# Six-stage transformer kernel: layer norms row tile by row tile, with their deviations made by GpSimd

## The reference

```
ln(x)  = (x - mean(x)) / sqrt(var(x) + 1e-5)        # over the last axis
x = x + L0_xattn(ctx, ctx, ln(x), mask, ...)        # 16 heads of 32, masked cross attention
x = x + L0_attn(ln(x), ...)                         # ln again with gain g and bias b, selective scan
x = x + L0_ffn(ln(x), ...)                          # shared expert and 2 of 8 experts
x = x + L1_xattn(ln(x), ctx, ctx, ...)              # 16 heads of 32, cross attention
x = x + L1_attn(ln(x), ...)                         # linear attention with cos and sin positions
x = x + L1_ffn(ln(x), ...)                          # see below
# L1_ffn(x): qkv = x @ w_qkv; causal attention o; h = ln(x + o) * g1 + b1
#            2 of 8 experts give moe; return ln(h + moe) * g2 + b2
```

## Time and profile before

| | |
|---|---|
| median of 3 runs | 4477.82 us (4474.61 to 4483.54) |
| the profiled execution's own time | 4484.0 us |
| its span | 4481.9 us |
| mean granted TensorE clock | 0.93 of full |
| busy: TensorE, VectorE, ScalarE, GpSimd | 3975.0, 2993.9, 2351.9, 1667.8 us |

### The profile page before, as it was taken

The page is one execution under the profiler, slowest core; times in us unless marked ns, Lnnn a source line. Parts: engine busy times, 40 slices in busy tenths (PEclk is TensorE's granted clock), DMA queues, the critical chain, the costliest instruction groups (busy, mean ns, idle before and its releaser), DMA issues. The chain is left out here.

```text
span 4481.9 us, 50984 instructions
## 1 busy us (share of the span) xinstructions
PE 3975.0 (89%) x17680; PEld 2213.4 (49%) x17680; DVE 2993.9 (67%) x3608; ACT 2351.9 (52%) x3611; POOL 1667.8 (37%) x984
## 2 busy tenths in 40 slices
PE   7995899999999686678999779999999988769997
PEld 6883344444443341147777434444444335447775
DVE  4333878777785359936777567777778644467776
ACT  2221577777777333313676426666666631337674
POOL 0001487778878425400000036666566630000000
PEclk9997899999999779889999869999999988789998
DMA  8998566666666200022888546666666540318886
GB/s 310 328 336 273 150 153 152 155 154 148 156 149 144 80 14 0 0 85 113 302 301 302 203 132 154 152 154 152 140 151 144 120 99 26 79 59 305 304 300 227
DMA packets 301550, 751.69 MB, mean 168 GB/s; under 512 B 55793, under 2 KB 89329, under 8 KB 268016
## 3 DMA queue, kind: packets, MB, share of 16 engines
q1 hardware_dynamic: 245136, 560.20, 37.1%
q0 software_dynamic: 47456, 171.46, 19.0%
q10 hardware_dynamic: 8704, 16.78, 1.1%
HBM read 484.23 MB, written 98.37 MB: 130 GB/s over the span
## 5 line engine op out<-in xcount | busy, mean ns | idle before, releaser
L749 ACT ACTIVATE prob<-psum 128x512 f32<-128x512 f32 x1552 | 891.7, 595 | 430.7 <-PE psum L647 393.7
L647 PE MATMUL psum<-q_stack,k_ring 98*128 98x512 f32 x2048 | 1006.1, 510 | 19.8 <-ACT prob L749 14.4
L924 POOL TENSOR_TENSOR den_pool<-den_pool,prob 128x1024 f32<-128x1024 f32 x372 | 937.2, 2519 | 220.2 <-DVE den_pool L836 184.7
L622 PE MATMUL psum<-k_ring,q_stack 96*128 96x512 f32 x2048 | 691.7, 422 | 106.3 <-DVE row_max L807 36.1
L803 DVE TENSOR_REDUCE row_max<-psum 128x1 f32<-128x1024 f32 x512 | 615.3, 1220 | 238.0 <-PE psum L622 235.0
L807 DVE CUSTOM_DVE_ANT_0 psum<-psum,mask_q 128x1024 f32<-128x1024 f32 x512 | 627.3, 1233 | 206.5 <-PE psum L622 191.2
L647 PEld LDWEIGHTS psum<-q_stack,k_ring 98*128 98x128 f32 x2048 | 395.2, 194 | 620.7 <-ACT prob L749 274.7
L1891 DVE TENSOR_TENSOR weight_lo<-weight_raw,weight_hi 128x2048 fp32r<-128x2048 f32 x240 | 546.9, 2289 | 163.2 <-ACT weight_hi L1834 162.9
L665 PE MATMUL psum<-prob,x 128*32 128x512 f32 x3104 | 515.7, 610 | 0.9 <-ACT prob L749 0.9
L622 PEld LDWEIGHTS psum<-k_ring,q_stack 96*128 96x128 f32 x2048 | 394.1, 200 | 213.7 <-issue 84.2
L1834 ACT ACTIVATE weight_hi<-weight_raw 128x2048 fp32r<-128x2048 f32 x240 | 454.4, 1916 | 43.2 <-DMA weight_raw<-in_L_ffn_w 25.3
(11 more groups left out here) (422 smaller groups left out, 6385.6 us busy)
## 6 DMA issues: line engine op xcount, KB each, us to landing
weight_raw<-in_L_ffn_w SPq DMA_DIRECT2D x120, 1024.0 KB, 6.7
den_dma<-prob POOLq DMA_DIRECT2D x204, 512.0 KB, 4.9
k_ring<-k_hi SPq DMA_DIRECT2D x1024, 64.0 KB, 2.2
weight_raw<-in_L_ffn_Wu SPq DMA_DIRECT2D x60, 1024.0 KB, 7.2
weight_raw<-in_L_ffn_Wd SPq DMA_DIRECT2D x60, 1024.0 KB, 4.9
den_dma<-xnT POOLq DMA_DIRECT2D x68, 512.0 KB, 4.9
k_ring<-k_lo SPq DMA_DIRECT2D x512, 64.0 KB, 2.4
ctxT<-in_ctxT SPq DMA_DIRECT2D x16, 1024.0 KB, 9.5
```

The source lines that it names most:

```text
L622: ins = e.matmul(max_banks(q)[:, a * KC:(a + 1) * KC], q_stack[h % n_q][0:QROWS, i * P:(i + 1) * P], k_ring[0:QROWS, (n + a) % kring, :], ...
L647: e.matmul(k.bank(b % 2), k_ring[:, n % kring, kt * P:(kt + 1) * P], q_stack[h % n_q][:], start=not masked, stop=True, skip_group_check=ma ...
L749: e.activation(prob[b // 2 % n_p][:, b % 2, :], k.bank(b % 2), ACT.Exp, scale=scale).then_inc(s_exp, 1)
L924: e.tensor_tensor(den[:], den[:], tile, ALU.add).then_inc(s_dpool, 1)
```

## The change

Each norm works row tile by row tile. GpSimd makes the deviation of a tile, as (var + eps) to the power -0.5, so that ScalarE's Sqrt and VectorE's reciprocal go. VectorE's list interleaves statistics, aggregates and rows of neighbouring tiles. TensorE transposes a row tile (its four squares into one bank) as soon as that tile is there; ScalarE, and in the context preparation and the scan input VectorE as before, copies the bank into xnT with columns strided by chunk. Where gain and bias are applied on the way (scan input), VectorE's 4 copies of 128x512 become 16 of 128x128. The diff, cut:

```
-        v.tensor_scalar(self.rstd[:], self.mv[:, :, 1], 1e-5, None, ALU.add).then_inc(self.s_var, 1)
-    def act_root(self, a):
-        a.wait_ge(self.s_var, 1)
-        a.activation(self.rstd[:], self.rstd[:], ACT.Sqrt).then_inc(self.s_root, 1)
+    def pool_rstd(self, g):
         for i in range(TT):
+            g.wait_ge(self.s_mean, i + 1)
+            g.tensor_scalar(self.rstd[:, i:i + 1], self.mv[:, i, 1:2], 1e-5, None, ALU.add).then_inc(self.s_eps, 1)
+            g.wait_ge(self.s_eps, i + 1)
+            g.tensor_tensor(self.rstd[:, i:i + 1], self.rstd[:, i:i + 1], self.k.minus_half[:], ALU.pow
+                            ).then_inc(self.s_rstd, 1)
...
+    def dve_rows(self, v, dst, src, done=None):
+
+        def row(i):
+            v.wait_ge(self.s_rstd, i + 1)
             v.tensor_scalar(dst[:, i, :], src[:, i, :], self.mv[:, i, 0:1], self.rstd[:, i:i + 1], ALU.subtract,
                             ALU.mult).then_inc(self.s_rows, 1)
+        for i in range(2):
+            self.dve_stats(v, src, i, done)
+        for i in range(TT):
+            self.dve_mean(v, i)
+            if i + 2 < TT:
+                self.dve_stats(v, src, i + 2, done)
+            if i > 0:
+                row(i - 1)
+        row(TT - 1)
...
     def pe_turn(self, p, src):
 
-        p.wait_ge(self.s_rows, TT)
-        for c in range(DT):
-            if c >= 2:
-                p.wait_ge(self.s_xT, c - 1)
-            for i in range(TT):
-                ins = p.transpose(self.k.bank(c % 2)[:, i * P:(i + 1) * P], src[:, i, c * P:(c + 1) * P],
+        for i in range(TT):
+            p.wait_ge(self.s_rows, i + 1)
+            if i >= 2:
+                p.wait_ge(self.s_xT, i - 1)
+            for c in range(DT):
+                ins = p.transpose(self.k.bank(i % 2)[:, c * P:(c + 1) * P], src[:, i, c * P:(c + 1) * P],
                                   self.k.ident[:])
             ins.then_inc(self.s_turned, 1)
...
+    def act_turned(self, a, dst):
+
+        for i in range(TT):
+            a.wait_ge(self.s_turned, i + 1)
+            a.activation(dst[:, :, i * P:(i + 1) * P], self.turned(i), ACT.Copy).then_inc(self.s_xT, 1)
...
+    def dve_turned_gained(self, v, dst, gain):
+        for i in range(TT):
+            v.wait_ge(self.s_turned, i + 1)
+            for c in range(DT):
+                ins = v.tensor_scalar(dst[:, c, i * P:(i + 1) * P], self.turned(i)[:, c, :], gain[:, 0, c:c + 1],
+                                      gain[:, 1, c:c + 1], ALU.mult, ALU.add)
+            ins.then_inc(self.s_xT, 1)
```

`dve_rows_gained` is interleaved in the same way, with its first pass (`scaled`) right behind each tile's aggregate. The edits in the lists:

```
     # scan_inputs, GpSimd
+                first.pool_rstd(e)
+                second.pool_rstd(e)
                 for c in range(DT - 1):
                     e.wait_ge(s_whi, c + 1)
                     e.tensor_tensor(w_part[1][:, c, :], w[:, c, :], w_part[0][:, c, :].bitcast(F32), ALU.subtract
...
     # scan_inputs, VectorE
-                e.wait_ge(first.s_rows, TT)
-                second.dve_variance(e, xn)
-                second.dve_rows(e, xm, xn)
+                second.dve_rows(e, xm, xn, done=lambda i: e.wait_ge(first.s_rows, i + 1))
                 e.wait_ge(s_c, 64)
-                second.dve_turned(e, k.xnT, gain=col)
+                second.dve_turned_gained(e, k.xnT, col)
...
     # l1_cross, ScalarE
-                        norm.act_root(e)
                         e.wait_ge(s_wq3, 16)
                         for c in range(DT):
                             e.activation(wq[:, c, :].rearrange("p (h n) -> p h n", n=DH), wq3[:, c, :, 0:DH], ACT.Copy
                                          ).then_inc(s_wq, 1)
+                        norm.act_turned(e, k.xnT)
                         q.act(e)
...
     # l0_experts, ScalarE
-                    norm.act_root(e)
                     ex.act_first_split(e)
+                    norm.act_turned(e, k.xnT)
                     ex.act_x(e, norm.s_xT)
...
     # l1_linear, ScalarE: after the exponentials, ahead of the silu copies
+                norm.act_turned(e, k.xnT)
                 e.wait_ge(s_pairs, 2)
...
     # causal_projections, ScalarE
-                norm.act_root(e)
+                norm.act_turned(e, k.xnT)
...
     # causal_to_routes, ScalarE
                     bias.act(e)
-                    norm.act_root(e)
-                    e.wait_ge(norm.s_rows, TT)
+                    norm.act_turned(e, k.xnT)
                     rows.act(e)
```

More of the change, by code:

```diff
@@ L128, in _ @@
             e.memset(k.ones[:], 1.0)
+            e.memset(k.minus_half[:], -0.5)
             e.wait_ge(s_zero, 2)
@@ L170, in dve_rows, with dve_stats, dve_mean @@
-    def dve_rows(self, v, dst, src):
-        v.wait_ge(self.s_root, 1)
-        v.reciprocal(self.rstd[:], self.rstd[:]).then_inc(self.s_rec, 1)
-        v.wait_ge(self.s_rec, 1)
-        for i in range(TT):
+    def dve_stats(self, v, src, i, done):
+        if done is not None:
+            done(i)
+        v.bn_stats(self.stats[:, i, :], src[:, i, :]).then_inc(self.s_stats, 1)
+    def dve_mean(self, v, i):
+        v.wait_ge(self.s_stats, i + 1)
+        v.bn_aggr(self.mv[:, i, :], self.stats[:, i, :]).then_inc(self.s_mean, 1)
@@ L182, in dve_rows_gained, with scaled, row @@
+        row(TT - 1)
+    def dve_rows_gained(self, v, dst, src, gain, plus, done=None):
+        def scaled(i):
             v.scalar_tensor_tensor(out=src[:, i, :], in0=src[:, i, :], scalar=self.mv[:, i, 0:1], in1=gain,
                                    op0=ALU.subtract, op1=ALU.mult).then_inc(self.s_scaled, 1)
-        v.wait_ge(self.s_root, 1)
-        v.reciprocal(self.rstd[:], self.rstd[:]).then_inc(self.s_rec, 1)
-        v.wait_ge(self.s_rec, 1)
-        for i in range(TT):
+        def row(i):
+            v.wait_ge(self.s_rstd, i + 1)
@@ L190, in dve_rows_gained @@
                                    op0=ALU.mult, op1=ALU.add).then_inc(self.s_rows, 1)
-    def pe_turn(self, p, src):
-        p.wait_ge(self.s_rows, TT)
-        for c in range(DT):
-            if c >= 2:
-                p.wait_ge(self.s_xT, c - 1)
-            for i in range(TT):
-                ins = p.transpose(self.k.bank(c % 2)[:, i * P:(i + 1) * P], src[:, i, c * P:(c + 1) * P],
+        for i in range(2):
+            self.dve_stats(v, src, i, done)
+        for i in range(TT):
+            self.dve_mean(v, i)
+            if i + 2 < TT:
+                self.dve_stats(v, src, i + 2, done)
+            v.wait_ge(self.s_mean, i + 1)
+            scaled(i)
+            if i > 0:
+                row(i - 1)
@@ L341, in _ @@
                 e.memset(m4[:], 0.0).then_inc(s_clear, 1)
+                norm.pool_rstd(e)
             @block.scalar
@@ L1005, in _ @@
                         k.clear_old(e)
+                    @block.gpsimd
+                    def _(e):
+                        norm.pool_rstd(e)
                     @block.vector
@@ L1086, in _ @@
             def _(e):
-                first.dve_variance(e, k.x)
                 first.dve_rows(e, xn, k.x)
-                e.wait_ge(first.s_rows, TT)
-                second.dve_variance(e, xn)
-                second.dve_rows(e, xm, xn)
+                second.dve_rows(e, xm, xn, done=lambda i: e.wait_ge(first.s_rows, i + 1))
                 e.wait_ge(s_c, 64)
-                second.dve_turned(e, k.xnT, gain=col)
+                second.dve_turned_gained(e, k.xnT, col)
                 for c in range(DT):
@@ L1137, in _ @@
             def _(e):
-                first.act_root(e)
                 for c in range(DT):
```

54 lines of the change are left out of this document (16 added, 38 removed).

## The result

The change is slower. Over nine runs each the changed kernel has a median of 4496.59 us (4488.13 to 4505.9), the kernel before 4478.0 us (4472.78 to 4485.88); the ratio is 1.0036, interval 1.0024 to 1.0049, so +16 us (18.6 between the medians). I had forecast 4477 us and a range up to 4488; 0.12 was my chance for slower. The profiled execution took 4496.59 us, its span is 4494.9, its mean granted clock 0.928. The page of after answers to the earlier trace rows: TensorE is busy 13.6 us longer although it does the same matmuls, VectorE 11.6 us less, GpSimd 34.8 us more.

A forecast was written before the change was run, and what follows sets the result against it. TensorE, busy 89% of the span, was taken as the bound, so only its waits for norms counted. Gains in scan input and before the router, mostly given back elsewhere, summed to -0.9 us: 4477 us forecast, range 4469 to 4488.

The forecast's parts named there:

- if the two cross attentions [...] change their length: Sign of being wrong: the cross attentions, some 2,200 us together and untouched by the diff, change length.
- P: Context preparation: VectorE's wait for the root goes, but nothing ahead of TensorE waited for it; 0 us.
- S: Scan input, two norms: in_proj_lo subtractions start later, yet TensorE's fourth group starts sooner; -4.4 us.
- L: In each norm, time from a bn_aggr's end until VectorE may use the tile's deviation; taken as 0.6 us.
- X: Shared expert: ScalarE's copies of the transposes stand behind its weight casts, so TensorE starts later; +1.4 us.
- C: Second cross attention: ScalarE's copies stand behind its wq casts, in full on the path; +3.1 us.
- L, +2.2: Linear attention: ScalarE's copies follow its exponentials, so TensorE starts later, though a table load goes; +2.2 us.
- R: Residual norm before the router: transposes and copies run beside the rows, so logits start sooner; -3.1 us.
- Q: Causal projections: norm ready some 4 us sooner, but TensorE waits for the w_qkv load; 0 us.
- O: Output norm: same VectorE work as before the router, with the stores behind its rows; -0.1 us.
- GpSimd is too slow: Rival, all norms: GpSimd's latency sets the pace; +12.7 us at L of 2.0, +27 at 2.7; chance 0.10.
- code loading: Rival, GpSimd: add and power drive each other's code out in each of 36 tiles; roughly +150 us; chance 0.02.

The follow-up runs named there:

- E16: Kernel before with 32 unused bytes ahead of q_stack, so only the first attention's own buffers move; ratio 1.0018.
- E1: Kernel before with an unused 32-byte buffer ahead of x, shifting x and every later buffer; 4488.6 us, ratio 1.0021.
- E8: Kernel before with 32 unused bytes ahead of the buffers of the first cross attention and its context preparation only; 4490.36 us, ratio 1.0026.
- E9: Kernel before with the new norm in the context preparation alone, all addresses kept; 4480.48 us, ratio 1.0003.
- E3: Changed kernel with -0.5 inside each norm's deviation tile, so every buffer keeps its old address, one memset more per norm; 4490.68 us, ratio 1.0022.
- E4: As E3, but VectorE copies the transposes in shared expert, second cross attention and linear attention; 4477.53 us, ratio 0.9997 against before.
- E10: Kernel before with the new norm in shared expert, second cross attention and linear attention only, addresses kept; 4488.41 us, ratio 1.0025.
- E15: Changed kernel with 224 unused bytes ahead of the first attention's buffers, returning them to their 256-byte boundary; ratio 1.0009 against before.
- E13: Kernel before with 256 unused bytes ahead of the first cross attention's buffers; measured to cost nothing.

## Why the prediction was wrong

- **The step that failed** is the one that isn't there. The prediction costs each instruction of the change; of `minus_half` my description of the change says "One memset of `minus_half` (128x1, -0.5) is added at the start of the program", and I gave it no term. The memset is free; its 32 bytes are not. They move the ring, mask and context buffers of the first attention 32 bytes past a 256-byte boundary, and that costs 8 to 12 us in the kernel before (E16 1.0018, E1 1.0021, E8 1.0026), more than any of my terms. It takes the loads of the ring and masks from 318 to 290 GB/s, and TensorE waits for them. I had put "if the two cross attentions [...] change their length" among the signs of being wrong, without a cause for it.
- **P, 0**: right, as far as E9 tells (1.0003).
- **S, -4.4**: -2.3 at TensorE's fourth group, -3.2 over the stage. Every link was as described; L was mis-sized at 0.6 us. For the first tile it is 0.97 (the aggregate ends at 1540.03, the power at 1541.00); the later tiles also queue behind GpSimd's cycle of 1.02 us and have theirs after 1.3 to 1.5. My formula for a norm paced by GpSimd, 1.35 + 4L + 0.5, gives 5.9 for the cycle of 1.02 (measured 6.08) and 7.9 for 1.52 (8.05); what was wrong is that I let it begin at L = 1.4, while it passes the 5.0 us of VectorE's order from a cycle of 0.8 on. The two norms took 1.1 us each longer than I had taken, so the subtractions began 11.4 us after the start and not 9.4, and x_lo, which waits for them, came 2.1 us later: that is the whole difference. The 16 gain instructions with the transposes between took 5.27 us, not 3.7, but lie ahead of that wait and cost nothing.
- **X, +1.4**: TensorE started 18.49 us after the norm's start, before 17.00: +1.5. **C, +3.1**: 3.34 us behind the casts instead of 0.05, though the weight landed 1.4 us sooner in that run (1.9 us later in all). **L, +2.2**: 13.99 us after the norm's start, before 12.48: +1.5. So the starts bear the terms out, but E3 against E4 and E10 show 9 to 13 us where I had 6.7. In the stage lengths the surplus is in the linear attention (+4.6 in the mean of four, with 147.0 among them). There the same small matmuls take 0.71 or 1.22 us by the clock granted, and the length follows the stage's mean clock in the old code too (table at E10): at 0.83 the old norm has 149.1 us and ScalarE's copies 150.0, at 0.85 145.7 to 147.0 and 147.0. I had no term for the clock. That a late start lowers it is not shown.
- **R, -3.1**: -2.4; the last row ends 8.87 us after the start (8.46 before), with the 0.46 us wait for GpSimd's pair that is slowed beside VectorE's two-input passes. **Q, 0**: right; TensorE's projections start 10.49 us after the norm's start, before 10.55. My 1.27 us there count from the end of the last transpose, not of its copy, which ends 0.5 us before TensorE starts. **O, -0.1**: +0.3 (12.6 against 12.3 us).
- **The rivals.** "GpSimd is too slow" had its latency term half right (L 0.97, a cycle of 1.02, not 1.7) and did not decide; code loading did not come. Its price was misread: the earlier trace rows show one line's records, and the program before has another such pair at 1.3 us; and the 3.2 us behind the pair at 495.6 end with VectorE's addition, for which GpSimd waits. In after the same instruction waits as long with no such record near it. VectorE and GpSimd before, GpSimd after:

```profile
497.42 1.22 DVE L836 TENSOR_TENSOR den_pool<-den_pool,prob 128x1024 f32<-128x1024 f32 x1
498.79 2.37 POOL L924 TENSOR_TENSOR den_pool<-den_pool,xnT 128x1024 f32<-128x1024 f32 x1 [3.21 <-DVE den_pool L836]
```

```profile
506.25 2.37 POOL L960 TENSOR_TENSOR den_pool<-den_pool,xnT 128x1024 f32<-128x1024 f32 x1 [3.09 <-DVE den_pool L872]
```

  So no run here gives a price for loading code. The result is on the slower side for a reason that neither rival had.

Summed with the means of the stage table: preparation +2.5, first attention +8.2, scan -3.2, shared expert +1.8 to +3.6 (with and without the 126.9), second attention's start +2.2, linear attention +4.6, router -2.4, so +14 to +15.5, against the measured +16. That the two agree is in part luck: the second cross attention, left out as untouched, scatters by more than the sum.

## What to carry to other kernels

Compare the allocation map before costing a diff: one small buffer ahead of large ones shifts them all, and where transfers bind (here the first 80 us of an attention) their rate may fall by 9%. Put small constants behind the large buffers, in the slack of a small one (E3), or pad back to the boundary (E15). When a copy moves to an engine that works its list in order, its price is read at the end of what stands ahead of it there, and with two banks it is paid as copy, transposes, copy.

## What the runs showed of the hardware

- Loads into SBUF buffers that start 32 bytes past a 256-byte boundary, with all DMA engines busy: 289 to 290 GB/s (four kernels), 299 at 64 bytes past it, 311 at 128, and 314 to 323 on it (12 kernels). The Trainium skill (DMA: Bandwidth & Descriptors, How a descriptor splits into AXI transactions) says that a transaction starts at a 256-byte-aligned address and that a descriptor that starts elsewhere costs beats for the bytes in front of it. E8 against E13 agrees that the start counts. By that rule of the Trainium skill, as an estimate, 2 KB cost 64 beats on the boundary, 65 at 32 bytes past it and 68 at 128; the runs show the opposite order and 9% instead of 2%, so the measurement decides and the rule doesn't explain the size. Why 128 bytes cost almost nothing stays open.
- GpSimd on 128x1 in after: an add 0.22 us and a power 0.57 where no row pass of VectorE was running at its start; a power 0.72 to 0.86 where a one-input row pass was (scan input), 0.92 where a two-input pass was (residual norm).
- A one-input VectorE instruction (the last row of xm, 0.55 us alone) was held 4.73 us by a GpSimd subtraction that began 0.07 us before it.
